# Generation of a state-space kernel: lag phases on ACT, a cosine from the half-angle sine, products on GpSimd, and an order for each engine

## The reference, cut to what matters

```python
dt = jnp.exp(log_dt)
A = A_re + 1j * A_im
C = C_re + 1j * C_im
dtA = dt[:, None] * A                       # 128 features x 64 states
dC = C * (jnp.exp(dtA) - 1.0) / A
powers = jnp.exp(dtA[:, :, None] * jnp.arange(L))   # L = 512 lags
K = 2.0 * jnp.einsum('dn,dnl->dl', dC, powers).real
...
y = jnp.fft.irfft(xf * Kf.T[None], n=n, axis=1)[:, :L]
return y + x * D_skip
```

## Time and profile before

| | us |
|---|---|
| median of 3 runs (lowest, highest) | 411.92 (411.9, 414.21) |
| the profiled execution, its own time | 411.81 |
| its span in the profile | 410.0 |
| PE busy | 312.0 (76%) |
| DVE busy | 279.1 (68%) |
| ACT busy | 214.1 (52%) |
| POOL busy | 106.5 (26%) |

### The profile page before, as it was taken

One profiled execution on the slowest core, in us unless ns is written; L12 is line 12 of the kernel. 1 busy time (PEld: TensorE's weight loads), 2 busy tenths in 40 slices (PEclk: granted clock), 3 DMA queues, 4 the chain that ended last, 5 costly groups with the idle time before them and its releaser, 6 DMA issues.

```text
span 410.0 us, 5286 instructions
## 1 busy us (share of the span) xinstructions
PE 312.0 (76%) x1518; PEld 156.5 (38%) x1518; DVE 279.1 (68%) x1219; ACT 214.1 (52%) x438; POOL 106.5 (26%) x172
## 2 busy tenths in 40 slices
PE   3310018097655899999989898979999999979895
PEld 1100015083342467745645333535444345223341
DVE  4997299998999889989587982482324457150353
ACT  4999505521305550399533468444777825717352
POOL 0599701216412846730340130040000000000000
PEclk9855558666959698899999999998999999678987
DMA  8910000000000000000000000000000000000001
GB/s 269 409 72 0 0 2 2 2 2 0 0 1 1 1 2 1 0 2 1 0 0 2 2 1 2 1 0 2 0 2 0 1 27 0 2 0 2 26 0 51
DMA packets 2625, 9.05 MB, mean 22 GB/s; under 512 B 548, under 2 KB 549, under 8 KB 2341
## 3 DMA queue, kind: packets, MB, share of 16 engines
q1 hardware_dynamic: 2596, 8.72, 5.6%
HBM read 7.67 MB, written 1.05 MB: 21 GB/s over the span
## 4 chain that ended last, share of the span: by engine, by line
PE 45%; DVE 14%; ACT 6%; issue 3%; DVEq 0%
PE bank L415 44%; DVE MT L957 3%; DVE R L1054 3%; ACT L731 2%; DVE V L1047 2%; DVE arena L957 2%; ACT arena L734 2%; ACT RS L734 1%; ACT pack_bfly L734 1%; DVE LO L957 1%; DVE XG L957 1%; DVE sel L987 0%; DVE pack_bfly L957 0%; DVE sm L991 0%; ACT E L734 0%
## 5 line engine op out<-in xcount | busy, mean ns | idle before, releaser
L731 ACT ACT_TABLE_LOAD x30 | 38.5, 1283 | 49.7 <-PE bank L415 24.0
L734 ACT ACTIVATE arena<-bank 128x512 f32<-128x512 f32 (+3 forms) x75 | 38.2, 569 | 17.7 <-PE bank L415 16.9
L734 ACT ACTIVATE E<-bank,negm 128x77 f32<-128x77 f32 x64 | 15.5, 326 | 55.6 <-DVE negm L961 55.6
L1054 DVE MATCH_REPLACE8 R<-V,R 128x77 f32<-128x77 f32 x192 | 40.5, 222 | 0.0
L1020 DVE TENSOR_REDUCE pack_bfly<-bank 128x4 f32<-128x308 f32 x64 | 26.0, 469 | 19.6 <-PE bank L415 19.6
L415 PE MATMUL bank<-arena 128*32 128x16 f32 (+3 forms) x304 | 12.7, 215 | 34.7 <-DVE arena L957 34.7
L1331 POOL TENSOR_TENSOR k0bd<-sel,w 128x308 f32<-128x308 f32 x16 | 11.3, 709 | 86.3 <-DVE w L961 86.1
L1047 DVE MAX8 V<-R 128x8 f32<-128x77 f32 x192 | 31.2, 224 | 0.0
L415 PE MATMUL bank<-pack_dft,arena 128*128 128x256 f32 x64 | 20.0, 482 | 12.8 <-DVE arena L957 12.8
L415 PE MATMUL bank<-arena,pack_dft 128*128 128x256 f32 (+1 forms) x96 | 29.3, 455 | 0.2 <-issue 0.2
L415 PE MATMUL bank<-LO,pack_first 128*128 128x512 f32 x48 | 26.1, 640 | 2.8 <-ACT LO L734 2.8
(11 more groups left out here) (202 smaller groups left out, 698.4 us busy)
## 6 DMA issues: line engine op xcount, KB each, us to landing
pack_bfly<-in_bfly SPq DMA_DIRECT2D x1, 2420.0 KB, 10.8
pack_dft<-in_dft SPq DMA_DIRECT2D x1, 1536.0 KB, 14.2
X<-in_x SPq DMA_DIRECT2D x4, 256.0 KB, 12.9
out_x<-X SPq DMA_DIRECT2D x4, 256.0 KB, 2.0
pack_ffn<-in_ffn SPq DMA_DIRECT2D x1, 512.0 KB, 14.9
pack_first<-in_first SPq DMA_DIRECT2D x1, 474.0 KB, 4.5
pack_moe<-in_moe SPq DMA_DIRECT2D x1, 452.0 KB, 15.6
pack_att<-in_att SPq DMA_DIRECT2D x1, 413.0 KB, 15.2
```

Of the source, the lines that this page charges most:

```text
L731: nc.scalar.add_instruction(mybir.InstLoadActFuncSet(name=nc.get_next_instruction_name(), act_func_set_id=need, ins=[], outs=[]))
L734: return nc.scalar.activation(out, in_, func, **kw)
L1054: nc.vector.match_replace(R8[:, g % 2, r % 2, h, :], V8[:, g % 2, h, r, :], src, NEG)\
```

## The change: what it does

The single list becomes four, one for each engine, and the index lists that semaphores count by (`CENTERED`, `SQUARED`, `SUMMED`, `VARS`) are taken from the list of the engine that does the counted thing. Banks are given out along PE's list. The generation is cut into more steps:

- the 16 high phases are ACT Copies (`s_qlag`), as the low ones; the DVE product and `l2row` go;
- DVE wraps the high phase once (`s_qarg`) and not twice; ACT takes the sine of half the angle and of the whole, and makes the cosine as 1 - 2*sin^2 with a Square and an Identity of 128x2048 (`s_qsin`, `cos_q`);
- the two products with be and al are POOL's (`s_qal`, `q_scaled`); DVE waits for them in `s_qc`;
- exponentials, sines and products are steps of their own (`s_qexp`, `s_pexp`, `s_psin0` to 3, `s_parg0` and 1, `s_pc0` to 3), and so are the ratio's tanh and sines (`s_trig`) and the low phases (`s_plag`);
- some steps get a wait that the common order made needless: `xt/0` and `film_pre/0` of ACT for `qc_done`, `dft/0` for `kern_ready`, `s_wup` and `s_wdn` for `freq_ready`.

The diff, cut to its core (of the four lists, the part that covers the generation and batch 0):

```diff
-KGEN, N_KGEN = columns([("logdt", D), ("are", D), ("aim", D), ("c1", D), ("c2", D), ("l2row", L2)])
+KGEN, N_KGEN = columns([("logdt", D), ("are", D), ("aim", D), ("c1", D), ("c2", D)])
...
+ORDER = {
+    "pe": """
+        center0/0 s_k0 var0/0 weigh0/0 s_pc0 s_m0 score0/0 center0/1 score1/0 weigh1/0 var0/1 s_vw score2/0 vw/0
+        s_w1 weigh2/0 score3/0 s_kern0 s_trig weigh3/0 s_ufly attnT/0 s_kern1 s_kern2 s_kern3 film_in/0 s_pexp
+        s_psin0 score0/1 weigh0/1 s_freq xt/0 score1/1 weigh1/1 dft/0 s_parg0 s_t1 s_qsin center0/2 s_wup mix/0
+        s_qarg weigh2/1 s_qexp score2/1 vw/1 weigh3/1 film_pre/0 top2/0 idft/0 score3/1 center1/0 var0/2 vw/2
+        center0/3 s_bup s_plag score0/2 film_out/0 var1/0 attnT/1 film_in/1 film_pre/1 xt/1 score1/2 dft/1 ffn_up0/0
+        ffn_up1/0 ffn_down/0 weigh0/2 score2/2 var2/0 vw/3 idft/1 s_t2 score3/2 center2/0 film_out/1 center1/1
+        weigh1/2 center3/0 s_qlag s_wdn x1/0 var3/0 s_dfly weigh2/2 top2/1 k1/0 var1/1 s_consts weigh3/2 var0/3
...
+    "act": """
+        s_kgen0 s_qlag center0/0 var0/0 s_m0 center0/1 s_vw score0/0 var0/1 s_trig score1/0 s_plag score2/0 s_qexp
+        s_qsin s_psin0 s_psin1 s_cols score3/0 vw/0 s_pexp s_psin2 s_psin3 s_kern1 attnT/0 s_kern3 score0/1 s_freq
+        xt/0 dft/0 s_t1 s_wup score1/1 vw/1 film_pre/0 center0/2 score2/1 score3/1 var0/2 center1/0 vw/2 var1/0
+        score0/2 attnT/1 xt/1 film_pre/1 dft/1 score1/2 ffn_up0/0 ffn_up1/0 center2/0 vw/3 var2/0 score2/2 s_t2
...
+    "dve": """
+        s_consts s_kgen0 s_masks s_k0 s_qarg var0/0 s_coef score0/0 score1/0 score2/0 s_w1 s_parg0 var0/1 score3/0
+        s_parg1 weigh3/0 s_qc s_pc0 s_pc1 s_pc2 s_pc3 s_cols s_kern1 s_kern3 film_in/0 score0/1 score1/1 mix/0
+        score2/1 film_pre/0 film_out/0 score3/1 var0/2 weigh3/1 s_bup score0/2 film_in/1 film_pre/1 var1/0 score1/2
+        mix/1 score2/2 var2/0 film_out/1 x1/0 score3/2 var3/0 var1/1 weigh3/2 var0/3 score0/3 film_in/2 fold_down/0
...
+    "pool": """
+        s_ufly s_coef weigh0/0 weigh1/0 s_qal weigh2/0 weigh3/0 var0/0 var0/1 s_udense mix/0 weigh0/1 s_dfly
+        weigh1/1 weigh2/1 weigh3/1 var0/2 s_dhigh mix/1 s_dlow weigh0/2 weigh1/2 weigh2/2 s_v1 k1/0 weigh3/2 mix/2
...
+SCHEDULE = {engine: [(step, int(b or 0)) for step, _, b in (word.partition("/") for word in words.split())]
+            for engine, words in ORDER.items()}
+CENTERED = [x for x in SCHEDULE["pe"] if x[0].startswith("center") and x[0] != "center2"]
+SQUARED = [x for x in SCHEDULE["act"] if x[0].startswith("center")]
+SUMMED = [x for x in SCHEDULE["pe"] if x[0].startswith("var")]
+VARS = [x for x in SCHEDULE["act"] if x[0].startswith("var")]
...
-    for at, (step, b) in enumerate(SCHEDULE):
+    for step, b in SCHEDULE["pe"]:
...
+                elif step == "s_trig":
+                    act.wait_ge(s["a_ready"], 1)
                     act.wait_ge(s["v_ready0"], 1)
                     a(kt["th"], kt["a"], ACT.Tanh, scale=0.5)
                     a(kt["sb"], kt["v"], ACT.Sin, scale=6.283185)
                     a(kt["q"], kt["v"], ACT.Sin, scale=3.1415925).then_inc(s["trig_ready"], 1)
-                elif step == "s_kgen1":
+                elif step == "s_plag":
+                    act.wait_ge(s["v_ready0"], 1)
                     for l in range(L1):
                         last = a(by_lag(big[0], L1)[:, l, :], kt["v"], ACT.Copy, scale=float(l))
                     last.then_inc(s["phase_p"], 1)
-                elif step == "s_kgen2":
+                elif step == "s_qlag":
+                    act.wait_ge(s["w_ready"], 1)
+                    for l in range(L2):
+                        last = a(by_lag(big[2][:, 2048:4096], L2)[:, l, :], kt["w"], ACT.Copy, scale=float(l))
+                    last.then_inc(s["phase_q"], 1)
+                elif step == "s_qsin":
                     act.wait_ge(s["consts_ready"], 1)
-                    for i, c in enumerate((big[2][:, 2048:4096], big[2][:, 0:2048])):
-                        act.wait_ge(s["arg_q"], i + 1)
-                        a(c, c, ACT.Sin, scale=6.283185, bias=(0.0, cst[:, 2:3])[i]).then_inc(s["sin_q"], 1)
-                elif step == "s_kgen3":
+                    act.wait_ge(s["arg_q"], 1)
+                    c, x = big[2][:, 0:2048], big[2][:, 2048:4096]
+                    linked(a(c, x, ACT.Sin, scale=3.1415925))
+                    a(x, x, ACT.Sin, scale=6.283185).then_inc(s["sin_q"], 1)
+                    settle()
+                    linked(a(c, c, ACT.Square))
+                    settle()
+                    a(c, c, ACT.Identity, scale=-2.0, bias=cst[:, 2:3]).then_inc(s["cos_q"], 1)
+                elif step == "s_qexp":
+                    act.wait_ge(s["a_ready"], 1)
                     for l in range(L2):
                         last = a(by_lag(big[3][:, 2048:4096], L2)[:, l, :], kt["a"], ACT.Exp, scale=float(L1 * l))
                     last.then_inc(s["exp_q"], 1)
+                elif step == "s_pexp":
+                    act.wait_ge(s["a_ready"], 1)
                     for l in range(L1):
                         last = a(by_lag(big[1], L1)[:, l, :], kt["a"], ACT.Exp, scale=float(l))
                     last.then_inc(s["exp_p"], 1)
-                elif step == "s_kgen4":
-                    for i, c in enumerate(QUARTERS):
-                        act.wait_ge(s["arg_p"], i + 1)
-                        a(big[0][:, c], big[0][:, c], ACT.Sin, scale=6.283185, bias=part("small", "sin_bias"))\
-                            .then_inc(s["sin_p"], 1)
+                elif step.startswith("s_psin"):
+                    c = QUARTERS[tile]
+                    if tile == 0:
+                        act.wait_ge(loaded["small"], 16)
+                    act.wait_ge(s["arg_p"], tile + 1)
+                    a(big[0][:, c], big[0][:, c], ACT.Sin, scale=6.283185, bias=part("small", "sin_bias"))\
+                        .then_inc(s["sin_p"], 1)
...
+                elif step == "s_qarg":
+                    x, turns = big[2][:, 2048:4096], big[3][:, 0:2048]
+                    dve.wait_ge(s["phase_q"], 1)
+                    chain(ts(turns, x, MAGIC, None, ALU.add))
+                    stt(x, turns, MAGIC, x, ALU.subtract, ALU.subtract, reverse1=True).then_inc(s["arg_q"], 1)
                     dve.wait_ge(s["arg_q"], 1)
-                    chain(ts(turns, ph, 0.25, MAGIC, ALU.add, ALU.add))
-                    stt(ph, turns, MAGIC, ph, ALU.subtract, ALU.subtract, reverse1=True).then_inc(s["arg_q"], 1)
...
+                elif step.startswith("s_parg"):
+                    half, turns = tile, big[3][:, 0:2048]
...
-                elif step == "s_kgen4":
-                    al, be = (kt[x].unsqueeze(2).broadcast_to([P, D, L2]) for x in ("al", "be"))
-                    as3 = lambda t: t.rearrange("p (d l) -> p d l", d=D)
-                    dve.wait_ge(s["sin_q"], 2)
-                    dve.wait_ge(s["ab_ready"], 1)
-                    linked(tt(as3(big[2][:, 2048:4096]), as3(big[2][:, 2048:4096]), be, ALU.mult))
-                    linked(tt(as3(big[2][:, 0:2048]), as3(big[2][:, 0:2048]), al, ALU.mult))
-                    settle()
+                    if half == 0:
+                        dve.wait_ge(loaded["small"], 16)
+                    else:
+                        dve.wait_ge(s["arg_p"], 2)
+                    chain(ts(turns, big[0][:, 2048 * half:2048 * half + 2048], part("small", "sin_off"), MAGIC,
+                             ALU.add, ALU.add))
+                    for c, at in ((QUARTERS[2 * half], 0), (QUARTERS[2 * half + 1], 1024)):
+                        stt(big[0][:, c], turns[:, at:at + 1024], MAGIC, big[0][:, c], ALU.subtract, ALU.subtract,
+                            reverse1=True).then_inc(s["arg_p"], 1)
+                    dve.wait_ge(s["arg_p"], 2 * half + 2)
+                elif step == "s_qc":
+                    dve.wait_ge(s["q_scaled"], 2)
                     chain(tt(big[3][:, 0:2048], big[2][:, 0:2048], big[2][:, 2048:4096], ALU.subtract))
                     dve.wait_ge(s["exp_q"], 1)
                     tt(big[3][:, 2048:4096], big[3][:, 0:2048], big[3][:, 2048:4096], ALU.mult).then_inc(s["qc_done"], 1)
-                elif step == "s_kgen5":
+                    dve.wait_ge(s["qc_done"], 1)
+                elif step.startswith("s_pc"):
+                    c = QUARTERS[tile]
                     dve.wait_ge(s["exp_p"], 1)
-                    for i, c in enumerate(QUARTERS):
-                        dve.wait_ge(s["sin_p"], i + 1)
-                        tt(big[0][:, c], big[0][:, c], big[1][:, c], ALU.mult).then_inc(s["p_done"], 1)
+                    dve.wait_ge(s["sin_p"], tile + 1)
+                    tt(big[0][:, c], big[0][:, c], big[1][:, c], ALU.mult).then_inc(s["p_done"], 1)
...
+                elif step == "s_qal":
+                    al, be = (kt[x].unsqueeze(2).broadcast_to([P, D, L2]) for x in ("al", "be"))
+                    as3 = lambda t: t.rearrange("p (d l) -> p d l", d=D)
```

(24 more changed lines are left out.)

101 lines of the change are left out of this document (59 added, 42 removed).

## The result

The changed kernel takes 374.01 us (median of 4 runs, 373.86 to 374.73) against 411.91 us for the kernel before beside it (410.84 to 414.21): a ratio of 0.9076, 95% interval 0.9036 to 0.9117. The profiled execution took 373.9 us, its span 372.1.

What follows compares the result with a forecast made beforehand. DVE was taken to bound the first 134.4 us, PE and DVE together the next stretch, PE the last; span 410.0 - 10.4 (shift) - 5 (moved work) = 394.6, plus 1.8 = 396.4, forecast 396 us, range 384 to 406.

Steps and rivals of the forecast that it cites:

- the first stretch: The kernel before up to 134.4 us, where PE's full stretch began; DVE was taken to set it.
- the walk: Step-by-step timing of the new lists in the first stretch: generation ends at 70.3, mix begins at 95.4, 13.8 us earlier.
- The rival of a slow POOL: In the generation, POOL's two products last 27 us or more and eat the gain; 425 us at 10 ns an element; chance 0.05.
- The wait moves from POOL to ACT's exponentials: In the generation, DVE's low quarters wait for ACT, so the generation ends at 70.3, not at 62.8.
- The rival of head-of-line waits: s_wup ahead of score1/1's exponentials on ACT and s_freq ahead of score1/1 on PE eat the gain: 406 us; chance 0.13.
- Step 1: First stretch, walked with the earlier profile's durations: PE's full stretch begins at about 124 instead of 134.4, a shift of 10.4 us.
- the first rival: Denser PE gets the higher clock early, shift 13 to 15, and all 9.5 us of moved work count: 387 us; chance 0.25.
- Step 2: Late lists after 134.4: order alone can give at most PE's 18.6 us of idleness; taken as zero.
- PE's idle time after 124: Sign in the new profile: forecast wrong if it differs from 18.6 + 5 us by more than 8.
- Step 3: Full stretches: 9.5 us of PE work (s_wup, s_bup, center0/3) brought forward counts half, 5 us.
- 6.1, 4.5 and 10.9 us of DVE's time: DVE's early savings: high phases 6.1, two broadcast products 4.5, wait for POOL's coefficients 10.9; at most 21.5 us together.

Runs made afterwards that it cites:

- e4_fold_late: Changed kernel with the weight folds s_wup and s_bup alone put back where the old order had them: 391.38 us, ratio 0.9515.
- e2_old_late: Changed kernel up to score0/2, with s_wup, s_bup and center0/3 in their new places, and the old common order from there: 395.57 us, ratio 0.9655.
- e7_fold_late_pool: Changed kernel with s_wup and s_bup back in their old-order places and POOL's s_dhigh moved behind mix/1: 379.15 us, ratio 0.9219.
- e1_common: Changed kernel's new generation, but all four engines walk the old common list: 412.1 us, ratio 1.0048 to the kernel before.
- e6_old_content: Changed kernel's four lists, with the old phases, cosine and products of the generation taken back: 382.08 us, ratio 0.9271.
- these mixtures: e12_mid_new and e13_mid_old, the changed kernel with part of its late lists in the old order: medians 391.87 and 390.35 us.
- e12_mid_new: Changed kernel's new lists until units0/0 of the old order, the old common order from there: median 391.87 us, runs 384.12 to 394.73.
- e13_mid_old: Changed kernel with the old common order from score0/2 to units0/0, new lists before and behind: 390.35 us, ratio 0.9469.
- e9_fill_center: Changed kernel with extra overwritten matmuls in PE's waits, four ahead of center1/0 and one ahead of film_in/1: median 372.99 us, runs 366.76 to 375.59.

## Why the prediction was wrong

Faster by over 1% was right at 0.87; the time was missed by 22 us: 6.8 in the first stretch and 15.7 behind it.

**What held.** The mechanism of the first stretch: DVE with all of batch 0's tiles where it had waited; POOL's products covered (ended 54.8; 60.7 in the walk); `s_freq` near the time of the walk (77.5, walk 75.9); the end of the generation at 71.0 (70.3); 27 table loads; DVE's wait for `s_qc` gone. The rival of a slow POOL fell, its products took 7.3 us and not 27. The added waits cost nothing that shows. "The wait moves from POOL to ACT's exponentials" was wrong without consequence: ACT ended at 66.4, and DVE never waited for it in `s_pc`. The rival of head-of-line waits fell too, as put (`s_wup` took 3.60 us, as in the full stretch before, and `s_freq` less than before); a wait of that kind was there on POOL's queue, one step away (`e4_fold_late`).

**Step 1, durations at the lower clock: shift 17.2, not 10.4.** I walked through a denser PE with the durations of a sparser one. `s_freq` at 8.24 us and a DVE wait of 5 us before `score1/1`: they were 6.03 and none, and the mix began at 91.4 instead of 95.4. Then `idft/0` 6.20 and `s_wup` up to 7.2 for what took 3.69 and 3.60: `film_out/0` ended at 106.6 instead of 113.5. This is the 6.8 us, and it is the first rival's mechanism ("a denser PE gets the higher clock"), to which I gave 0.25 and 15 us at most.

**Step 2, "the loss has no such bound, and I take zero": the late orders were worth 13.9 us with the folds in place, 20.0 with the folds moved.** This is the step that failed: a term of zero without a reason. The bound set beside it was badly reasoned. I took "idle PE time after 134.4 ... 18.6 us" as all that order can give, as if busy time were fixed. With the folds in place the number held, but only 5.7 of the 13.9 us were idleness and 8.2 a higher clock for the same matmuls. And the old late order, after the folds had left it, had 27.1 us of idleness, so moving work out makes idleness that only order removes: there the gain went over the bound, 13.4 us of idleness and 6.6 of busy time. PE's idle time after 124, one of the signs, was 11.8 us (248.1 less 236.3 busy) where 23.6 was forecast, outside the 8 us that I had allowed. The change has four new lists; I costed 117 us of them with a walk and the remaining 255 with a zero. One sign was in sight: the granted clock of 0.94 and 0.93 in the late windows of the earlier trace rows said that the 18.6 us of gaps might be costing more than themselves.

**Step 3, moved work counts half, 5 us.** It is worth 0.7 us in the old late order (275.6 to 274.9, `e2_old_late`); in the new one it takes 6.8 us off the late stretch, and 5 of 7.8 us are left by the medians (`e7_fold_late_pool`). That the number was near is luck, for the reason was wrong: what share of moved work counts depends on whether something else is ready to follow.

**Content and order.** The prediction priced parts of the content one by one (6.1, 4.5 and 10.9 us of DVE's time) and added them under the new list, which was right only because the list was there: without it they give 0 (`e1_common`), with it 8 (`e6_old_content`). The 10.9 us wait was a matter of the list alone.

**What stays open.** Which engine's list makes the late gain wasn't tried. That the middle gives 9.6 us and the end 8.0 is shown by one profile each; the medians of these mixtures give less. Whether `e9_fill_center`'s 7 us can be had steadily is open.

## What to carry to other kernels

Don't cost a reordering at zero because the sum of work stays: read the granted clock in each stretch that it touches. Where it is under 1, PE's busy time is a result of the gaps too, and durations for a denser timeline are to be taken from rows at full clock. A gain in one stretch and an order that can use it belong together: measure them as a two-by-two (content or order, early or late) before you drop either, for one alone may show nothing. And of a step that is moved, look at every queue for what waits on it: 12 of 17 us hung on one POOL step.
